# First block of a conditioned residual model: the order of shift, scores and value products on TensorE

## The chip, the cores and the metric

The kernel runs on one core of one Trainium2 chip. The metric is the device time of one execution in microseconds (us). A core has TensorE (PE in the profile, with its weight loads as PEld), VectorE (DVE), ScalarE (ACT), GpSimd (POOL) and SyncE (SP, which here only issues DMAs). Each runs its own list of instructions in order, and they meet through semaphores: an instruction's `then_inc` raises one, a `wait_ge` holds an engine's list until a value is reached.

## The reference

The input x is 16 x 128 x 256. Two layers are added to it in turn.

The first is a masked self-attention in which queries, keys and values are the same projection:

```
x  = x + L0(x, cond)        # 8 heads of 16 channels, T = 256 columns, per batch
  q      = xt @ Wq.T                       # xt: x with its last two axes swapped
  scores = scale * q q^T                   # 256 x 256 per batch and head
  logits = (scores*cmask + (1-cmask)*NEG) * rmask
  ctx    = softmax(logits) q ;  out = ctx @ Wo.T
x  = x + L1(x, cond, ...)   # adaptive layer norm, attention with 16 heads of 128, MLP with gelu
```

The second is a transformer block with modulations computed from cond. It takes most of the time and the change does not touch it.

## The kernel before, in words

`build` runs two parts one after the other: `first_block` (the first layer, and beside it the preparation of the second layer's weights, modulations and first layer norm) and `layers` (the second layer). Each part is written as one list of instructions per engine, and the order in each list is written out by hand.

`first_block` works in 32 units, numbered n = 0 to 31. A unit is two heads (s = 0, 1) of two batches (b = 0, 1). Four units make a group: a group g is the two batches 2g and 2g+1 with all eight heads. The unit's 2 x 2 score tiles live in the four PSUM banks of `ring`: bank 2b + s. So half b of a unit uses banks 2b and 2b+1, and the next unit uses the same banks again.

For half b of unit n:

- `scores(n, b)` (line 446, PE) writes the raw, masked scores of both heads for both key tiles. It waits until the exponentials of unit n-1 have read the same banks (`act_exp`), and at the first unit of a group for the operands QS and KS to be gathered (`l_q`).
- `maxima(n, b)` (line 678, DVE) takes the negated maxima of the two banks, one instruction for each bank.
- `shift(n, b)` (line 458, PE) adds these to the scores in PSUM, by multiplying the maxima with an identity. It waits for `dve_max`, bank by bank.
- `exponentials(n, b)` (line 611, ACT) writes `pt`, one instruction for each bank. `pt` has two buffers, so it waits for the value products of unit n-2 (`pe_pv`).
- `pv(n, kt)` (line 470, PE) is one half (a key tile kt) of the unit's value products: `V` against `pt`, into a 32-row band of the PSUM tile O (`pair`) for each batch and head. It comes a unit late, as `pv(n - 1, ...)` in step n, and needs all four exponentials of its unit (`act_exp` 4n).

The tensor list's step n is: `scores(n, 0)`, `shift(n-1, 1)`, then work that comes once a group, then the first product of unit n-1, `shift(n, 0)`, `scores(n, 1)`, and the second product of unit n-1. The ScalarE list's step n is: `exponentials(n-1, 1)`, copies that come once a group, one cast of 512 columns of the second layer's weights (`w_hi`, line 647, in steps 2 to 25), `exponentials(n, 0)`. In VectorE's list it is `maxima(n, 0)`, group work, `maxima(n, 1)`.

The work once a group, by n mod 4, is this. In steps 0 and 1, ScalarE copies a half of the last group's O (line 619). In steps 1 and 2, PE transposes these (line 514), and VectorE divides by the sums. In step 2, PE projects the queries of the group after next (line 790 with `wq_h`), ScalarE copies them (`qh`, line 594) and VectorE forms their low part (`ql`, line 673). In step 3, PE transposes the contexts (line 521) and projects the next group's values (line 395), which ScalarE copies (line 601). In step 0 PE multiplies with Wo (line 526), and VectorE adds to X (line 772).

The operands of a group go through DRAM. SP stores `qh` and `ql` to `qd` (`gather`, lines 281 and 283), and later, once they have landed, loads them in stacked form into QS and KS (`spread`, line 299). Between these SP loads masks (`mb`, line 272) and weight chunks (`stage`, line 307), the latter when GpSimd is done with the chunk two before.

At steps 28 and 29 ScalarE also computes the row sums and squares of the first layer norm of the second layer (lines 124 and 141), after `exponentials(n, 0)`. After the last unit, PE computes the modulations (line 404), and the last group's contexts are finished.

Of the kernel before, what the change touches and what calls it, by code (L numbers as in the profile page):

```python
# [16 lines left out]
UNITS = B // 2 * 4  # L17
# [26 lines left out]
def wait(eng, sem, value):  # L44

    if not isinstance(value, int) or value > 0:
        eng.wait_ge(sem, value)
# [125 lines left out]
def first_block(nc, sem, sb, x, cond, Wq, Wo, ada_w, ada_b, qkv_w, qkv_b, out_b, ffn_b1, ffn_b2,  # L173
# [10 lines left out]
    with ExitStack() as ctx:  # L184
# [67 lines left out]
        def nth(g):  # L252

            return (g + 1) // 2

        def tail_of(n, lag):

            g, r = divmod(n - lag, 4)
            return g if r == 0 and 0 <= g < NGR else None

        with nc.Block() as block:
# [119 lines left out]
            def _(pe):  # L381
                def project(g):

                    wait(pe, pool_x, g)
                    wait(pe, act_v, g - 1)
                    products(nc, vbank[:, :], lambda k: wq_h[:, :], lambda k: wq_l[:, :], lambda k: xh[:, :],
                             lambda k: xl[:, :], True, True, range(1)).then_inc(pe_q, 1)

                def values(g):

                    taken = min(g + 1, NGR - 1)
                    wait(pe, act_q1, taken)
                    wait(pe, dve_ql, taken)
                    for bk in range(4):
                        last = nc.tensor.matmul(vbank[:, bk * P:(bk + 1) * P],
                                                X[:, 2 * g + bk // 2, bk % 2 * P:(bk % 2 + 1) * P], wT[:, 0, :],
                                                start=True, stop=True)
                    last.then_inc(pe_v, 1)
# [33 lines left out]
                def scores(n, b):  # L432

                    g, j = divmod(n, 4)
                    if g == 0 and b == 0:
                        pe.wait_ge(dve_st, j + 1)
                    elif j == 0 and b == 0:
                        pe.wait_ge(l_q[g % 2], LQ * nth(g))
                    if n == 0 and b == 1:
                        pe.wait_ge(dve_set, 2)  # L440
                    wait(pe, act_exp, 4 * (n - 1) + 2 * b + 2)
                    for kt in range(2):
                        for s in range(2):
                            r = slice(64 * s, 64 * s + ROWS_ONE + 1)
                            k0 = b * 256 + kt * P
                            last = nc.tensor.matmul(ring[:, 2 * b + s, kt * 256:kt * 256 + 256],  # L446
                                                    KS[r, g % 2, j, k0:k0 + P], QS[r, g % 2, j, b * 256:b * 256 + 256],
                                                    start=(kt == 0), stop=True, skip_group_check=True)
                            if kt == 1:
                                last.then_inc(pe_s, 1)  # L450

                def shift(n, b):

                    for s in range(2):
                        wait(pe, dve_max, 4 * n + 2 * b + s + 1)
                        for qt in range(2):
                            out = ring[:, 2 * b + s, :].rearrange("p (k q) -> p k q", k=2)[:, :, qt * P:(qt + 1) * P]
                            last = nc.tensor.matmul(out, mx[:, 2 * b + s, qt:qt + 1].to_broadcast([P, P]),  # L458
                                                    identr[:, None, :].to_broadcast([P, 2, P]),
                                                    start=False, stop=True, skip_group_check=True)  # L460
                        last.then_inc(pe_sh, 1)

                def pv(n, kt):

                    g, j = divmod(n, 4)
                    col = j % 2 * 256
                    for b in range(2):
                        for s in range(2):
                            row = (2 * s + b) * HP
                            last = nc.tensor.matmul(O[row:row + HP, j // 2, col:col + 256],  # L470
                                                    V[:, g % 2, b * 2 + kt, 2 * j + s, :],
                                                    pt[:, n % 2, b, s, kt * 256:kt * 256 + 256],
                                                    start=(kt == 0), stop=(kt == 1))
                    if kt == 1:
                        last.then_inc(pe_pv, 1)
# [16 lines left out]
                for n in range(LAST + 1):  # L492
                    if n < UNITS:
                        scores(n, 0)
                    if 0 <= n - 1 < UNITS:
                        shift(n - 1, 1)
                    if n == 0:
                        pe.wait_ge(act_set, 1)
                        pe.wait_ge(dve_set, 1)
                        project(1)  # L500
                    if n < 3:
                        stack(n + 1)

                    for t in range(2):
                        g = tail_of(n, 5 + t)
                        if g is not None:
                            wait(pe, act_o, 2 * g + t + 1)
                            if t == 0:
                                wait(pe, dve_x, g)
                            else:  # L510
                                wait(pe, dve_ctx, 2 * g + 1)
                            for qt in range(2):
                                for jj in range(2):
                                    last = nc.tensor.transpose(tbank[:, (2 * qt + jj) * P:(2 * qt + jj + 1) * P],
                                                               oT[:, t, (2 * jj + qt) * P:(2 * jj + qt + 1) * P], ident)
                            last.then_inc(pe_oT, 1)
                    g = tail_of(n, 7)
                    if g is not None:
                        wait(pe, dve_ctx, 2 * g + 2)
                        for i in range(4):  # L520
                            last = nc.tensor.transpose(tbank[:, i * P:(i + 1) * P], ctxs[:, i, :], ident)
                        last.then_inc(pe_ctxT, 1)
                    g = tail_of(n, 8)
                    if g is not None:
                        wait(pe, act_ctxT, g + 1)
                        nc.tensor.matmul(tbank[:, :], wT[:, 1, :], ctxT, start=True, stop=True).then_inc(pe_out, 1)
                    if n % 4 == 2 and n // 4 + 2 < NGR:
                        project(n // 4 + 2)
                    if n % 4 == 3 and n // 4 + 1 < NGR:
                        values(n // 4 + 1)  # L530

                    if 0 <= n - 1 < UNITS:
                        if (n - 1) % 4 == 0:
                            wait(pe, act_v, (n - 1) // 4 + 1)
                        if (n - 1) % 2 == 0:
                            wait(pe, act_o, (n - 1) // 2 - 1)
                        wait(pe, act_exp, 4 * n)
                        pv(n - 1, 0)
                    if n < UNITS:
                        shift(n, 0)  # L540
                        scores(n, 1)
                    if n == 0:
                        values(0)
                    if 0 <= n - 1 < UNITS:
                        pv(n - 1, 1)
                    if n == UNITS:
                        pe.wait_ge(act_exp, 4 * UNITS)
                        pe.wait_ge(l_small, 80)
                        nc.tensor.transpose(ring[:, 1, 12 * B:12 * B + BIASES], bias_rows, ident[0:BIASES, 0:BIASES])
                        pe.wait_ge(l_ada, 48)  # L550
                        for part in range(4):
                            modulations(part)
                    if n == UNITS + 1:

                        pe.wait_ge(dve_n1, 1)
                        pe.wait_ge(act_exp, 4 * UNITS)
                        for half in range(2):
                            transposed(nc, ident, normal, half, (vbank, ring[:, 0, :])[half]).then_inc(pe_n1, 1)
# [941 lines left out]
```

## Time and profile before

| | us |
|---|---|
| median of 3 runs | 788.14 |
| lowest, highest | 786.65, 790.93 |
| profiled execution | 792.2 |
| its span in the profile | 790.0 |

The first block takes the span up to about 198 us; the layers take the rest. In the rows below, a line of the timeline merges neighbouring instructions of one kind (x4 is four of them), and gives the start of the first and the time from there to the end of the last. An idle time in brackets stands with what ended it. Lines marked PEld are weight loads. A "..." stands where lines are left out.

### The profile page before, as it was taken

What the parts mean: (1) busy time and instruction counts of PE and PEld (TensorE: products, weight loads), DVE (VectorE), ACT (ScalarE), POOL (GpSimd) and SP (SyncE); (2) the same over time, 40 slices, a digit from 0 to 9 for tenths busy, and PEclk for the clock granted to TensorE, in tenths of its full rate; (3) what the DMA queues carried; (4) which work ended last, traced back from release to release, by engine and by line L of the source; (5) the groups of instructions that cost most, each with busy time, mean ns of one, the idle gap of its engine ahead of it and who ended that gap; (6) DMA issues with size and microseconds to landing.
All of it is one profiled execution on the core that took longest, in us unless ns stands there. A gap on an engine that the chain in (4) does not pass through costs nothing.

```text
span 790.0 us, 12978 instructions
## 1 busy us (share of the span) xinstructions
PE 756.6 (96%) x4763; PEld 621.5 (79%) x4763; DVE 394.5 (50%) x801; ACT 439.5 (56%) x1194; POOL 142.5 (18%) x133
## 2 busy tenths in 40 slices
PE   7799999986999999999999999999999999899997
PEld 4455555555888888888988888988898888778886
DVE  5656666664235534444545443555544435446444
ACT  2557767671465554455655447465454485557653
POOL 4134443100232111111111111111111223200000
PEclk9979999995899999999999999999999999999999
DMA  3989888701332221221212212212222232221001
GB/s 114 180 214 208 214 193 190 143 27 47 126 121 94 68 81 67 68 81 54 80 64 72 80 66 66 71 62 80 81 68 69 69 117 94 67 80 40 30 12 53
DMA packets 67707, 73.30 MB, mean 93 GB/s; under 512 B 3936, under 2 KB 47960, under 8 KB 67656
## 3 DMA queue, kind: packets, MB, share of 16 engines
q1 hardware_dynamic: 67192, 72.40, 32.6%
q8 instruction: 32, 0.52, 0.3%
q10 hardware_dynamic: 464, 0.22, 0.1%
q14 instruction: 19, 0.16, 0.1%
HBM read 46.36 MB, written 26.25 MB: 92 GB/s over the span
## 4 chain that ended last, share of the span: by engine, by line
PE 70%; DVE 3%; ACT 2%; DMA 1%; issue 0%; DVEq 0%; SPq 0%; ACTq 0%
PE bank L790 27%; PE pair L790 14%; PE ring L790 13%; PE ring L1076 7%; PE pair L1062 7%; PE ring L116 1%; DVE x1l L1304 1%; ACT x1h L1164 1%; PE ring L1095 0%; ACT probs L1183 0%; DMA x1f<-in_L_cond_ffn_w_dram 0%; PE ring L1031 0%; DVE ol L1337 0%; DVE pB L1315 0%; DMA turned<-pB 0%
## 5 line engine op out<-in xcount | busy, mean ns | idle before, releaser
L1183 ACT ACTIVATE probs<-pair,nm 128x128 f32<-128x128 f32 x256 | 98.2, 485 | 183.7 <-DVE nm L1326 183.7
L1439 POOL TENSOR_TENSOR probs<-probs,rinv 128x512 f32<-128x512 f32 x64 | 66.6, 1041 | 357.0 <-DVE rinv L1334 357.0
L790 PE MATMUL bank<-x1h,w_hi 128*128 128x512 f32 x256 | 112.1, 438 | 5.6 <-DVE x1l L1304 5.5
L678 DVE TENSOR_REDUCE mx<-ring 128x2 fp32r<-128x512 f32 x128 | 79.8, 683 | 45.1 <-PE ring L446 45.1
L790 PE MATMUL bank<-x1l,w_hi 128*128 128x512 f32 x256 | 101.5, 396 | 0.0
L790 PE MATMUL bank<-x1h,w_lo 128*128 128x512 f32 x256 | 101.3, 396 | 0.0
L611 ACT ACTIVATE pt<-ring 128x512 f32<-128x512 f32 x128 | 70.3, 595 | 45.0 <-PE ring L458 45.0
L1357 DVE COPY Vv<-pair 128x512 f32<-128x512 f32 x64 | 44.2, 691 | 81.0 <-PE pair L790 81.0
L790 PE MATMUL pair<-w_hi,x1l 128*128 128x256 f32 x256 | 72.8, 284 | 0.0
L790 PE MATMUL pair<-w_lo,x1h 128*128 128x256 f32 x256 | 72.6, 283 | 0.0
L790 PE MATMUL pair<-w_hi,x1h 128*128 128x256 f32 x256 | 72.3, 282 | 0.0
L1076 PEld LDWEIGHTS ring<-pT,Vv 128*128 128x128 f32 x512 | 67.7, 193 | 5.2
L1062 PEld LDWEIGHTS pair<-K,Q 128*128 128x128 f32 x512 | 67.0, 191 | 5.3
L1076 PE MATMUL ring<-pT,Vv 128*128 128x128 f32 x512 | 68.2, 276 | 0.0
L1062 PE MATMUL pair<-K,Q 128*128 128x128 f32 x512 | 67.6, 275 | 0.0
L1337 DVE SCALAR_TENSOR_TENSOR ol<-ring,bias,oh 128x512 fp32r<-128x512 f32 x64 | 48.1, 751 | 33.8 <-ACT oh L1192 33.8
L1326 DVE TENSOR_REDUCE nm<-pair 128x4 f32<-128x512 f32 x64 | 43.6, 682 | 40.3 <-PE pair L1062 40.0
L1334 DVE RECIPROCAL rinv<-sums 128x4 f32<-128x4 f32 x64 | 11.4, 178 | 102.0 <-ACT probs L1183 102.0
L790 PEld LDWEIGHTS bank<-x1h,w_hi 128*128 128x128 f32 x256 | 49.1, 192 | 13.6 <-issue 6.6
L790 PEld LDWEIGHTS bank<-x1h,w_lo 128*128 128x128 f32 x256 | 48.6, 190 | 11.0
L1183 ACT ACTIVATION_READ_ACCUMULATOR probs<-pair,nm 128x1 f32 x256 | 56.0, 219 | 0.0
L458 PEld LDWEIGHTS ring<-identr,mx 128*128 128x128 f32 x256 | 37.6, 196 | 22.7 <-issue 13.4
(206 smaller groups left out, 1518.4 us busy)
## 6 DMA issues: line engine op xcount, KB each, us to landing
turned<-pB SPq DMA_DIRECT2D x63, 256.0 KB, 2.0
pT<-turned SPq DMA_DIRECT2D x63, 256.0 KB, 2.7
stage<-in_L_cond_qkv_w_dram SPq DMA_DIRECT2D x12, 512.0 KB, 9.5
QS<-qd SPq DMA_DIRECT2D x14, 384.0 KB
qd<-qh SPq DMA_DIRECT2D x14, 256.0 KB
KS<-qd SPq DMA_DIRECT2D x14, 256.0 KB
mb<-in_cond_dram SPq DMA_DIRECT2D x8, 256.0 KB, 9.6
kept<-X SPq DMA_DIRECT2D x1, 2048.0 KB, 8.0
```

The lines of the kernel that those rows point to most:

```text
L458: last = nc.tensor.matmul(out, mx[:, 2 * b + s, qt:qt + 1].to_broadcast([P, P]), identr[:, None, :].to_broadcast([P, 2, P]), start=False, ...
L611: nc.scalar.activation(pt[:, n % 2, b, s, :], ring[:, 2 * b + s, :], ACT.Exp, scale=DK ** -0.5).then_inc(act_exp, 1)
L678: dve.tensor_reduce(mx[:, 2 * b + s, :], ring[:, 2 * b + s, :].rearrange("p (k q) -> p k q", k=2), AX_X, ALU.max, negate=True).then_inc(dv ...
L790: last = nc.tensor.matmul(bank, w(k), x(k), start=(start and i == 0), stop=(stop and i == len(terms) - 1))
L1062: last = nc.tensor.matmul(Sb[:, t], Q[:, h % 2, t], K[:, h % 2, t], start=True, stop=True)
L1076: last = nc.tensor.matmul(Ob[:, b * T:(b + 1) * T], V[:, ho // 2 % 2, b, h % 2 * DH:(h % 2 + 1) * DH], pT[:, h % 2, :, b, :], start=True, ...
L1183: last = nc.scalar.activation(plain(probs)[:, t] if direct else probs[:, :, b, :].rearrange("p c a -> p a c"), Sb[:, t] if direct else Sb[ ...
L1326: dve.tensor_reduce(nm[:, h % 2, :], Sb[:, :].rearrange("p (b k) -> p b k", b=GB), AX_X, ALU.max, negate=True).then_inc(dve_mx, 1)
L1334: dve.reciprocal(rinv[:, h % 2, :], sums[:, h % 2, :]).then_inc(dve_ri, 1)
L1337: dve.scalar_tensor_tensor(ol[:, :], Ob[:, :], qkvb[:, 2, ho:ho + 1], oh[:, :].bitcast(F32), ALU.add, ALU.subtract).then_inc(dve_ol, 1)
L1357: dve.tensor_copy(V[:, hn // 2 % 2, 2 * (hn % 2):2 * (hn % 2) + 2, :], Vb[:, :].rearrange("p (b d) -> p b d", b=2)).then_inc(dve_v, 1)
L1439: pool.tensor_tensor(w, w, r, ALU.mult).then_inc(pool_p, 1)
```

## The change

In step n of the tensor list, `shift(n, 0)` and `scores(n, 1)` move ahead of the wait for the exponentials of unit n-1 and of the first value product; the second value product, which stood at the end of the step, moves up to stand directly behind the first. No instruction, semaphore or wait is added or taken out, and the other engines' lists are the same. The step is then: `scores(n, 0)`, `shift(n-1, 1)`, work once a group, `shift(n, 0)`, `scores(n, 1)`, both products of unit n-1.

```diff
--- before.py
+++ after.py
@@ -529,6 +529,9 @@
                     if n % 4 == 3 and n // 4 + 1 < NGR:
                         values(n // 4 + 1)
 
+                    if n < UNITS:
+                        shift(n, 0)
+                        scores(n, 1)
                     if 0 <= n - 1 < UNITS:
                         if (n - 1) % 4 == 0:
                             wait(pe, act_v, (n - 1) // 4 + 1)
@@ -536,13 +539,9 @@
                             wait(pe, act_o, (n - 1) // 2 - 1)
                         wait(pe, act_exp, 4 * n)
                         pv(n - 1, 0)
-                    if n < UNITS:
-                        shift(n, 0)
-                        scores(n, 1)
+                        pv(n - 1, 1)
                     if n == 0:
                         values(0)
-                    if 0 <= n - 1 < UNITS:
-                        pv(n - 1, 1)
                     if n == UNITS:
                         pe.wait_ge(act_exp, 4 * UNITS)
                         pe.wait_ge(l_small, 80)
```

## Rows read from the trace of the kernel before

**Rows 1.** The page, busy time, share and instructions of each engine.

```profile
PE 756.6 (96%) x4763; PEld 621.5 (79%) x4763; DVE 394.5 (50%) x801; ACT 439.5 (56%) x1194; POOL 142.5 (18%) x133
```

**Rows 2.** Windows; columns: stretch, length, busy (instructions) per engine, clock, DMA share, GB/s.

```profile
35.00:39.00 4.00, 0.30 (x10) 0.06 (x2) 1.00 (x2) 0.19 (x1) 0.50 (x1) 1.00 1.09 196
...
43.00:47.00 4.00, 4.00 (x24) 2.53 (x23) 2.50 (x4) 2.02 (x4) 3.19 (x4) 0.50 0.60 238
...
70.00:100.00 30.00, 29.15 (x245) 18.36 (x246) 20.13 (x40) 20.86 (x39) 12.01 (x10) 1.00 0.93 205
```

**Rows 3.** Timeline of a group's second unit; start, duration, engine, line, operation, [idle before].

```profile
83.65 2.48 DVE L678 TENSOR_REDUCE mx<-ring 128x2 fp32r<-128x512 f32 x4 [1.06 <-PE ring L446]
...
84.19 0.50 PE L446 MATMUL ring<-QS,KS 49*128 49x256 f32 x4
...
84.62 0.88 PE L458 MATMUL ring<-identr,mx 128*128 128x256 f32 x4
...
85.16 1.08 ACT L611 ACTIVATE pt<-ring 128x512 f32<-128x512 f32 x2 [1.02 <-PE ring L458]
...
85.34 0.60 PE L514 MATMUL bank<-cst,late 128*128 128x128 f32 x4
...
86.39 0.64 PE L470 MATMUL pair<-pt,V 128*32 128x256 f32 x8 [0.45 <-ACT pt L611]
...
86.95 0.73 PE L458 MATMUL ring<-identr,mx 128*128 128x256 f32 x4
...
87.56 1.09 ACT L611 ACTIVATE pt<-ring 128x512 f32<-128x512 f32 x2 [0.32 <-PE ring L458]
...
87.61 0.50 PE L446 MATMUL ring<-QS,KS 49*128 49x256 f32 x4
...
88.69 0.50 PE L446 MATMUL ring<-QS,KS 49*128 49x256 f32 x4
```

**Rows 4.** The same timeline, exponentials of the group's first unit.

```profile
83.05 1.08 ACT L611 ACTIVATE pt<-ring 128x512 f32<-128x512 f32 x2 [0.22 <-PE ring L458]
```

**Rows 5.** The same timeline, cast and exponentials of its third unit.

```profile
91.66 0.62 ACT L647 CAST w_hi<-stage 128x512 fp32r<-128x512 f32 x1
...
92.23 1.08 ACT L611 ACTIVATE pt<-ring 128x512 f32<-128x512 f32 x2
```

**Rows 6.** The same view over units 26 to 31.

```profile
148.41 1.09 ACT L611 ACTIVATE pt<-ring 128x512 f32<-128x512 f32 x2 [1.22 <-PE ring L458]
...
153.28 1.09 ACT L611 ACTIVATE pt<-ring 128x512 f32<-128x512 f32 x2 [0.47 <-PE ring L458]
...
154.51 0.50 PE L446 MATMUL ring<-QS,KS 49*128 49x256 f32 x4
...
157.78 1.09 ACT L611 ACTIVATE pt<-ring 128x512 f32<-128x512 f32 x2 [0.74 <-PE ring L458]
...
162.73 1.09 ACT L611 ACTIVATE pt<-ring 128x512 f32<-128x512 f32 x2 [0.83 <-PE ring L458]
...
168.04 1.08 ACT L611 ACTIVATE pt<-ring 128x512 f32<-128x512 f32 x2 [1.22 <-PE ring L458]
...
172.55 1.08 ACT L611 ACTIVATE pt<-ring 128x512 f32<-128x512 f32 x2 [0.84 <-PE ring L458]
...
174.43 1.19 ACT L611 ACTIVATE pt<-ring 128x512 f32<-128x512 f32 x2 [0.79 <-PE ring L458]
```

**Rows 7.** Timeline: two group heads and the mask load between them.

```profile
98.59 0.51 PE L446 MATMUL ring<-QS,KS 49*128 49x256 f32 x4
...
105.45 0.44 SPq L272 DMA_DIRECT2D mb<-in_cond_dram  x1
...
117.40 0.50 PE L446 MATMUL ring<-QS,KS 49*128 49x256 f32 x4
```

**Rows 8.** DMA issues in 98 to 108; columns: KB each, us from issue to landing.

```profile
mb<-in_cond_dram SPq DMA_DIRECT2D x1, 256.0 KB, 10.4
```

**Rows 9.** Waits of the DMA-issuing queue SP: us in total, times, longest.

```profile
SPq L299 <- DMA qd<-ql: 15.2, 7, 5.8
```

## The prediction

> **What bounds the kernel now.** I read the page first, then the stretches, then the timeline of the first block. On the page TensorE is busy for 96% of the span [rows 1], which seems to leave nothing to reorder. The stretches say the same of the first block (0.97 busy in 70 to 100), and add that the DMA engines are busy for 0.93 of it there [rows 2]. The timeline of one unit says what the busy share hides. I call a unit's blocks S0 and S1 (scores, line 446), T0 and T1 (shifts, 458), P0 and P1 (value products, 470), E0 and E1 (the two pairs of exponentials, 611). The reader is to follow starts, since they show when PE could go on:
>
> S0 84.19, T1 of the unit before 84.62, E1 85.16, four transposes 85.34, then P0 at 86.39 after 0.45 idle for E1, T0 86.95, E0 87.56, S1 87.61, and the next S0 at 88.69 [rows 3]. The next S0 starts 0.04 after E0 ends (87.56 + 1.09 = 88.65). So ScalarE's E0 ends the unit, and ScalarE itself stood idle 0.32 before E0, for T0. T0 had its maxima long before: those of S0 are the last two of the four reductions that start at 83.65; at 2.48 / 4 = 0.62 apart, the third, T0's first, is done near 85.6. T0 stood only behind P0, and P0 behind E1. The loop is E1, P0, T0, E0, S0, T1, E1, through two engines that wait for each other. PE is not the bound; its order is.
>
> **The change, part by part.**
>
> *No instruction is added or removed, and no wait.* All semaphore counts stay. S1's own wait for E1 (act_exp 4n) was satisfied by P0's before; now S1 is the one that waits, and P0 and P1 find it done. No DMA is moved; SP and POOL see only earlier counts.
>
> *T0 ahead of P0.* T0 can start once the transposes and its maxima are done, near 85.8 in the unit of rows 3, instead of 86.95. E0 can then follow the weight cast directly: the idle 0.32 goes. It is the same in the first unit of a group, where ACT idles 0.22 before E0 [rows 4]. In the third unit E0's row has no idle time at all [rows 5], nor has the fourth's: there, as the code's order has it, ScalarE is held by the query copy and the value copy, which wait for projections that stay where they are. These two units gain nothing. So a group gains 0.22 + 0.32 = 0.54 (the bounds: 0, if T0 is held by something else, and 0.45 more in the second unit, P0's own wait).
>
> *S1 ahead of P0 and P1.* S1 waits for E1 (ends 86.24), then P0 and P1 follow. P0 takes 0.57 (86.39 to 86.95), S 0.43 (84.19 to 84.62), T 0.66 (86.95 to 87.61). PE's own path through a unit is 2 x 0.43 + 2 x 0.66 + 2 x 0.57 = 3.3, with the transposes (0.4 to 0.6) 3.8. That is the price: both products now stand between S1 and the next S0. In the second unit of a group ScalarE needs 88.69 - 84.19 - 0.32 = 4.2, so 0.4 is spare. Where ScalarE has no cast or copy to do, the 3.8 becomes the bound and eats part of what the wait gave.
>
> *The two products together.* They no longer switch between kinds of matmul in between. No row of before shows an uninterrupted pair; the nearest, P0's 0.57 to the next block, bounds a pair at 1.14, and 0.43 (an S block's) would make it 1.00. From -0.14 to 0 a unit, and only where PE is the bound; I take 0.
>
> *Where it adds up.* Counted by unit (0 to 31):
> - Units 0 to 3 wait for the operand stacks on VectorE and then for the gathers; nothing. Units 4 to 7 run partly at half clock [rows 2], where PE's own path is the longer one: between 0 and 0.54, I take 0.2.
> - Units 8 to 23, four groups of 0.54: 2.2. Units 24 and 25: 0.5.
> - Units 26 and 27 have no cast; ACT idles 1.22 and 0.47 before E0 [rows 6]. PE's path caps this: the sum is 1.7 at most, 0 at least; unit 26 keeps some 0.7 and unit 27, which has the value projection on PE, some 0.2. I take 0.9.
> - Units 28 to 31, where the layer norm's sums and squares run on ScalarE between the exponentials: idle 0.74, 0.83, 1.22 and 0.84 before E0 [rows 6], 3.6 together. Every one of these waits is for T0 behind P0 behind E1. The last unit's products come after E1 as before, so what PE's path takes here falls mostly in the shade of the squares. I take 3.3; the ends are 2.3 (0.3 a unit to PE's path) and 3.6.
>
> Sum without transfers: 0.2 + 2.2 + 0.5 + 0.9 + 3.3 = 7.1.
>
> *What the faster loop runs into.* Each group's first S0 waits for gathers through DRAM. For the head at 117.40 the mask load, issued behind the gathers at 105.45, landed 10.4 later, at 115.85 [rows 7, 8]. The gathers should have landed by then, so 1.5 was left; the sum has taken 0.2 + 3 x 0.54 = 1.8 by that head and 3.8 by the head of unit 28. SP waited for the operands' stores to land in all 7 gathers, 15.2 in total [rows 9], so this chain of transfers is little helped by earlier compute, at 0.93 busy engines [rows 2]. If it moves not at all, 2.3 of the 3.8 is lost; if it moves along, 0. I take 1.0, nearer to moving, since the weight loads that share the engines are issued earlier as well. Sum: **6.1**.
>
> The Trainium skill ("DMA: Bandwidth & Descriptors", Queues, rings and completion order) says that each DMA engine takes descriptors in ring order but that completion isn't first in, first out per issuing engine. By it the bound of 115.85 is a likely one and no certain one; by the rows alone the 1.5 stays as it is.
>
> After unit 31 (modulations, transposes, the start of the layers) the chain moves as a whole; PE's clock there may change level a little earlier or later in it, 0.5 either way. The layers are untouched.
>
> The profiled execution took 792.2 (span 790.0 and 2.2 around it), 4.1 above the median of 788.14. 792.2 - 6.1 = 786.1 for it, and 782.0 for the median.
>
> **The rivals.**
>
> *A: the transfers take it all (chance 0.16).* The gathers hold every head, so units 4 to 27 end where they did, and only the tail's 3.3 is left: 784.8. For it: 0.93 busy DMA engines, SP's waits. Against: 1.5 was left at the head I could date, and no full-speed head shows a measured wait.
>
> *B: slower (0.07).* PE, done sooner, waits at the heads long enough to lose its clock. That has happened once: in 35 to 39 PE was busy for 0.30 of 4 us (the wait for the first gathers), and in 43 to 47 the clock was 0.50, the level of 1.2 GHz [rows 2]. At that level the path of 3.8 doubles to near 7.6 against units of 4.5, so one such head costs about 3 a unit and 6 in two units. That wait was 3.7, and I take the rival to decide from a wait of that order; the sum above has heads wait under 1.5. With two such heads and the tail's gain: 788.1 - 3.3 + 12 = 796.8; one, with the rest of A, makes 790.8, and I write 791 for the rival.
> The Trainium skill ("TensorE: Matmul & The Clock Gate", HAM oscillation) describes just this: a wait for transfers in each round throttles the array again every round. Here the trace agrees at the one long wait; by the rule this rival would strike wherever a wait is as long as that one.
>
> *C: the wait only moves (0.07).* S1 waits for E1 as P0 did, and P0 and P1 between S1 and S0 cost what T0 gained: 788. Against it: in the unit of rows 3, T0 at 85.8 puts S1 at 86.5 and the pair from 86.9 to 88.0, before E0 ends (88.65 - 0.32 = 88.3).
>
> *D: more than forecast (0.10).* Transfers move along, and units 26 and 27 give their whole 1.7 because the pair of products is cheap: 7.1 + 0.8 = 7.9; and where E0 follows a cast with no idle it starts 0.05 before the cast ends (92.23 against 91.66 + 0.62 [rows 5]), in ten units 0.5 more: 8.4, so 779.7.
>
> **How the numbers follow.** The forecast (gain 4.5 to 8, 0.60): 782.0. A median of this kernel can tell about 0.5%, 3.9, from no change. Faster by more: forecast and D, 0.70. Within: A and C, 0.23. Slower: B, 0.07. The range is from 778.5 (D, with a microsecond of spread) to 786.5 (A, with half a microsecond of clock and one of spread), and leaves C, B and the far side of D outside.
>
> **What would show it.** Right: ACT's idle time for line 458 falls in first and second units; PE waits for E1 at S1, none at P0; the distance of group heads (98.59 to 117.40, 18.81 [rows 7]) falls toward 18.3; E1 of the last unit starts some 6 earlier than 174.43 [rows 6]. In the third and fourth unit of a group nothing changes. Wrong: group heads that stay at 18.8 with PE waiting for DMA (A); a clock of 0.50 after a head (B); E0 as late as before although T0 is early (C). The tail's share can be read apart: from the S0 at 154.51 to E1 at 174.43 it is 19.92 now [rows 6], and should be near 16.6.

## The result, and the profile after

Nine runs of each kernel: 784.72 us after against 788.73 before, ratio 0.9924 with a 95% interval of 0.990 to 0.9948; that is 6.0 faster, between 4.1 and 7.9. The gains in this text come from these ratios; differences of the medians can be smaller, and here the two medians are only 4.0 apart. The forecast was a gain of 6.1 and a median of 782.0; the measured median is 2.7 above that, inside the stated range (778.5 to 786.5). One of the twelve executions of the kernel called "end alone" below took 1830.47, in a slow state, and is not in its ratio. The profiled execution took 785.6, with a span of 783.4, against 792.2 and 790.0.

The page of the kernel after, busy time of each engine. It looks like [rows 1]: PE's (TensorE's) busy share went from 96% to 95% while the kernel gained 6. The Trainium skill ("Perfetto Trace Analysis", Identifying the Most-Contended Engine) warns that matmul busy time is a poor measure of how close TensorE is to its limit; here the rows agree.

```profile
PE 745.7 (95%) x4763; PEld 623.4 (80%) x4763; DVE 396.4 (51%) x801; ACT 437.2 (56%) x1194; POOL 142.4 (18%) x133
```

The timeline after, a group's second unit. It answers to [rows 3]; columns as there.

```profile
64.35 0.50 PE L446 MATMUL ring<-QS,KS 49*128 49x256 f32 x4 [0.16 <-ACT pt L610]
...
64.79 0.74 PE L458 MATMUL ring<-identr,mx 128*128 128x256 f32 x4
...
65.32 1.09 ACT L610 ACTIVATE pt<-ring 128x512 f32<-128x512 f32 x2 [1.02 <-PE ring L458]
65.36 0.60 PE L514 MATMUL bank<-cst,late 128*128 128x128 f32 x4
...
65.72 1.02 PE L458 MATMUL ring<-identr,mx 128*128 128x256 f32 x4
...
66.66 0.50 PE L446 MATMUL ring<-QS,KS 49*128 49x256 f32 x4
66.76 0.64 ACT L646 CAST w_hi<-stage 128x512 fp32r<-128x512 f32 x1
67.10 1.07 PE L470 MATMUL pair<-pt,V 128*32 128x256 f32 x16
67.28 1.11 ACT L610 ACTIVATE pt<-ring 128x512 f32<-128x512 f32 x2
68.44 0.50 PE L446 MATMUL ring<-QS,KS 49*128 49x256 f32 x4 [0.28 <-ACT pt L610]
```

T0 starts at 65.72, right behind the transposes. E0 at 67.28 has no idle time before it; it starts 0.12 before the cast ends (66.76 + 0.64). The products are one block at 67.10 and lie beside E0. The unit is 4.09 long (64.35 to 68.44), where it was 4.50. E0's end still sets the next S0, and PE now has 0.28 idle there.

The first unit of the next group shows the other side. I call the first S0 of a group its head. Timeline after, then windows (columns as in [rows 2]):

```profile
76.68 1.07 PE L470 MATMUL pair<-pt,V 128*32 128x256 f32 x16
...
79.37 0.50 PE L446 MATMUL ring<-QS,KS 49*128 49x256 f32 x4 [1.62 <-DMA QS<-qd]
```

```profile
78.00:79.00 1.00, 0.00 (x0) 0.00 (x0) 0.07 (x1) 0.00 (x0) 0.34 (x1) 1.00 0.99 154
...
81.00:82.00 1.00, 1.00 (x3) 0.49 (x3) 0.35 (x2) 1.00 (x3) 0.91 (x2) 0.50 0.90 344
82.00:83.00 1.00, 1.00 (x8) 0.78 (x6) 0.54 (x1) 1.00 (x3) 0.95 (x1) 0.50 0.59 223
...
85.00:86.00 1.00, 1.00 (x11) 0.87 (x10) 0.70 (x2) 0.27 (x1) 0.00 (x0) 1.00 0.46 133
```

PE had nothing to do from 77.75 to 79.37; the gathers had not landed. Then its clock was at 0.50 (1.2 GHz) in 81 to 83 and at 1.00 again in 85 to 86, and the unit took 5.39 in place of 4.09. Before, no head but the first gathered one (38.95) waited for a transfer.

SP's wait for the stores to land is longer than in [rows 9]; waits of SP after:

```profile
SPq L299 <- DMA qd<-ql: 23.5, 7, 6.8
```

The issues themselves show what became of the earlier compute. First stores of a group's queries and the gathers that wait for them, timeline before, then after:

```profile
73.02 1.27 SPq L281 DMA_DIRECT2D qd<-qh  x2
...
84.00 0.81 SPq L299 DMA_DIRECT2D KS<-qd  x2
```

```profile
71.43 1.27 SPq L281 DMA_DIRECT2D qd<-qh  x2
...
84.85 0.81 SPq L299 DMA_DIRECT2D KS<-qd  x2
```

The stores were issued 1.6 earlier and the gathers 0.85 later. Over the five groups issued from 53 to 130, the time from the first store to the first gather was 10.0 to 11.8 before and 11.7 to 13.4 after.

The end of the block, timeline after (answers to [rows 6]):

```profile
153.07 0.50 PE L446 MATMUL ring<-QS,KS 49*128 49x256 f32 x4 [1.34 <-DMA QS<-qd]
...
162.70 2.03 ACT L610 ACTIVATE pt<-ring 128x512 f32<-128x512 f32 x4
...
169.53 1.08 ACT L610 ACTIVATE pt<-ring 128x512 f32<-128x512 f32 x2 [0.76 <-PE ring L458]
```

Unit 28's head gained 1.44 (154.51 to 153.07). From there to the last E1 it took 16.46, where it was 19.92, so 3.46 more. At 162.70 four exponentials stand in one row without idle time, E1 of unit 29 and E0 of unit 30: the squares of the layer norm hold ScalarE, and when they end both are ready.

Then the stretch from the modulations to the layers, which gives the last 1.5 of the 6.6 between the two spans. Windows of the kernel before and of the one after:

```profile
176.80:197.80 21.00, 14.47 (x75) 12.09 (x71) 9.15 (x34) 3.72 (x7) 0.00 (x0) 0.57 0.15 49
```

```profile
171.70:191.30 19.60, 13.03 (x76) 10.66 (x72) 9.22 (x34) 3.72 (x7) 0.00 (x0) 0.62 0.16 54
```

The same work with a mean clock of 0.62 against 0.57. By their starts (first modulation to first product of the layers) it was 176.89 to 197.84, and is 171.85 to 191.28: 1.5 shorter. PE's clock fell to 0.50 about 3 after the first modulation before, and about 4.5 after it here.

### The profile page after: what moved, and what is told of

The parts are those of the page before. It is cut to its first block, busy times and chain, and to the rows that moved or that the text cites. A ratio compares the mean times of both kernels' runs of the same rounds, so it can differ in the third digit from the quotient of the medians.

```text
span 783.4 us, 12978 instructions
## 1 busy us (share of the span) xinstructions
PE 745.7 (95%) x4763; PEld 623.4 (80%) x4763; DVE 396.4 (51%) x801; ACT 437.2 (56%) x1194; POOL 142.4 (18%) x133
## 4 chain that ended last, share of the span: by engine, by line
PE 70%; DVE 3%; ACT 2%; DMA 1%; issue 0%; DVEq 0%; SPq 0%; ACTq 0%
PE bank L789 28%; PE pair L789 14%; PE ring L789 13%; PE ring L1075 7%; PE pair L1061 7%; PE ring L116 1%; DVE x1l L1303 1%; ACT x1h L1163 1%; PE ring L1094 0%; ACT probs L1182 0%; DMA x1f<-in_L_cond_ffn_w_dram 0%; PE ring L1030 0%; DVE ol L1336 0%; DVE pB L1314 0%; DMA turned<-pB 0%
## 5 line engine op out<-in xcount | busy, mean ns | idle before, releaser
L677 DVE TENSOR_REDUCE mx<-ring 128x2 fp32r<-128x512 f32 x128 | 81.7, 685 | 37.4 <-PE ring L446 37.0
L458 PE MATMUL ring<-identr,mx 128*128 128x256 f32 x256 | 55.3, 329 | 1.8 <-DVE mx L677 0.5
```

The costliest lines, as they stand in the source:

```text
L677: dve.tensor_reduce(mx[:, 2 * b + s, :], ring[:, 2 * b + s, :].rearrange("p (k q) -> p k q", k=2), AX_X, ALU.max, negate=True).then_inc(dv ...
```

## The experiments

Each time is a median beside that of the kernel before on the same chip; the gain is the ratio's, and the medians themselves differ by up to 1.2 less. For the traces I give the heads of groups 2 to 7 (first S0 of units 8, 12, ..., 28) and the start of the last unit's S1. Before they are 60.96, 79.78, 98.59, 117.40, 136.21, 154.51 and 172.61; after 60.26, 79.37, 98.54, 116.39, 135.41, 153.07 and 167.56.

**Only T0 moved.**

```diff
+                    if n < UNITS:
+                        shift(n, 0)
                     if 0 <= n - 1 < UNITS:
...
                         pv(n - 1, 0)
                     if n < UNITS:
-                        shift(n, 0)
                         scores(n, 1)
```

> Only the first shift T0 stands ahead of the first value product; the second scores S1 stay between the two products. Theory 1 (the gain is E0 of the unit starting without waiting for P0 and E1): nearly all of the change's gain of 6.0 (0.76% of 788.7) is here, 4.5 to 6, since E0 needs T0 alone; in the trace ACT's idle time before E0 is gone in first and second units and a group's second unit is near 4.1 long. Theory 2 (S1 ahead and the closed pair of products carry a good part, because PE's own path and the maxima of S1 bound the units): 3 or less.

785.46 against 789.56, ratio 0.9939 (0.9915 to 0.9962): 4.8 faster. Timeline of its first and second unit behind a head:

```profile
83.97 1.00 PE L458 MATMUL ring<-identr,mx 128*128 128x256 f32 x4
...
84.90 0.64 PE L470 MATMUL pair<-pt,V 128*32 128x256 f32 x8
84.90 0.64 ACT L648 CAST w_hi<-stage 128x512 fp32r<-128x512 f32 x1
85.42 1.11 ACT L612 ACTIVATE pt<-ring 128x512 f32<-128x512 f32 x2
85.47 0.50 PE L446 MATMUL ring<-QS,KS 49*128 49x256 f32 x4
85.90 0.64 PE L470 MATMUL pair<-pt,V 128*32 128x256 f32 x8
86.58 0.50 PE L446 MATMUL ring<-QS,KS 49*128 49x256 f32 x4
```

E0 follows the cast as it does after, and the unit is 4.08 long: T0 ahead is the whole of it here. S1 and the closed pair are worth 0.1 in the third unit (4.57 against 4.48) and 0.16 to 0.3 in units without a cast (unit 26: 3.96 against 3.75; unit 28: 4.00 against 3.84; unit 30: 4.07 against 3.77). From unit 28's head to the last S1 this kernel took 15.72, the old order 18.10 and the change 14.49: of the tail's 3.6, T0 gives 2.4, and S1 with the pair 1.2. No run tells S1 from the pair. Theory 1 for the body, and for two thirds of the tail.

**Only the pair closed**, ahead of T0.

```diff
                         pv(n - 1, 0)
+                        pv(n - 1, 1)
                     if n < UNITS:
                         shift(n, 0)
                         scores(n, 1)
...
-                    if 0 <= n - 1 < UNITS:
-                        pv(n - 1, 1)
```

> The two products stand together, but ahead of T0 and S1, as the first did before. Theory 1: the pair (1.0 instead of 0.57) now lies between E1 and E0, 0.43 more in each ACT-bound unit, 28 units: 8 to 12 slower than before, 797 to 801. Theory 2 (the pair itself is worth something): within 3 of before.

799.99 against 789.56, ratio 1.0138 (1.0095 to 1.0182): 10.9 slower. Timeline, a group's first unit:

```profile
83.68 1.07 PE L470 MATMUL pair<-pt,V 128*32 128x256 f32 x16
...
84.68 0.73 PE L458 MATMUL ring<-identr,mx 128*128 128x256 f32 x4
85.27 1.08 ACT L610 ACTIVATE pt<-ring 128x512 f32<-128x512 f32 x2 [0.65 <-PE ring L458]
```

A pair takes 1.00 to the next block, 0.43 more than one product, and all of that is added to ScalarE's idle time: 0.22 [rows 4] became 0.65. So what PE does between E1 and E0 is on the path at full price.

**The end alone, and the rest alone.**

```diff
+                    early = n >= 28      # the other kernel: n < 28
+                    if early and n < UNITS:
+                        shift(n, 0)
+                        scores(n, 1)
...
                         pv(n - 1, 0)
-                    if n < UNITS:
+                    if not early and n < UNITS:
                         shift(n, 0)
                         scores(n, 1)
```

> The new order in steps 28 to 32 only, the old one before. Theory 1 (the tail of the block, where the layer norm's sums stand on ScalarE and no gathers are due, gives 3.6 as the two traces show): 3 to 4.5 faster than before, and the time from the head of unit 28 to the last exponentials as short as after. Theory 2 (the gain comes evenly from all units, 4 of 32): under 1.5.

> The new order in steps 0 to 27 only, the old one from 28. Theory 1 (the gathers hold the heads of the groups): 1 to 2 faster than before, head of unit 28 near 153, from there as before. Theory 2 (body and tail share the gain by the number of their units): 4 to 5 faster.

Theory 1 held for the end, and for the rest in its size but not in the head it named (near 153). End alone: 786.19 against 789.56, ratio 0.9949 (0.9926 to 0.9972), 4.0 faster. From unit 28's head to the last S1 it took 14.49, as after, where it was 18.10: 3.6 gained.

Rest alone: 788.20, ratio 0.9982 (0.9961 to 1.0003), 1.4 faster at best estimate and not told from nothing. Its heads: 59.92, 77.80, 95.67, then 114.81, 135.25, 154.27. After two groups of 17.9 it was 2.9 ahead of before, and the next three gave all but 0.2 back: two heads waited 1.65 and 2.55 for gathers, and behind the second wait PE ran at half clock. Timeline at that head, and the windows behind the two waits:

```profile
135.25 0.80 PE L446 MATMUL ring<-QS,KS 49*128 49x256 f32 x4 [2.55 <-DMA QS<-qd]
```

```profile
115.00:119.00 4.00, 3.74 (x34) 2.20 (x32) 3.21 (x5) 2.92 (x6) 2.21 (x3) 1.00 0.79 305
...
135.25:141.25 6.00, 6.00 (x26) 3.85 (x30) 2.71 (x5) 3.16 (x6) 1.28 (x1) 0.50 0.46 152
```

Unit 24, behind 135.25, took 6.84 in place of 4.09.

**Less transferred beside the gathers.** The two kernels leave out 7/8 of the qkv weights from the third chunk on, so the products of the layers use stale weights.

```diff
+                    w = CHUNK if c < 2 else 128
-                    sp.dma_start(stage[:, c % 2, :], qkv_v[:, k, n * CHUNK:(n + 1) * CHUNK])...
+                    sp.dma_start(stage[:, c % 2, 0:w], qkv_v[:, k, n * CHUNK:n * CHUNK + w])...
```

> Old order; from the third chunk on, the transfers of the qkv weights bring only 128 of 1024 columns (the rest of the product weights is left stale), so ten transfers of 512 KB shrink to 64 KB. If the old order is bound by the loop of engines and not by transfers at the heads of groups 3 to 7: the same distances of heads (18.8), total within 2 of before except for what the first gathers, which wait for transfers, give (0 to 2).

> New order with the same lightened weight transfers. Theory 1 (transfers hold the heads in the new order): PE's waits for gathers at the heads go, heads at 17.9 to 18.3 apart, and the gain over the light kernel in the old order is 7 to 8.5 instead of 6. Theory 2 (the gathers' own chain, not the weights beside it, or something else sets the heads): same distances as after, gain over the light old order near 6.

Old order: ratio 1.0003 (0.9974 to 1.0032), heads 18.8 apart as before. New order: 0.9854 (0.9803 to 0.9904), 11.5 faster; heads at 60.03, 79.20, 97.07, 114.94, 132.81, 149.07, with three distances of 17.87. Only the head at 60.03 waited for a gather (1.59), and its unit took 5.39. The gain over the light old order is 11.8 by these ratios, more than the 7 to 8.5 expected; why it is more stays open. The transfers held the new order and not the old one.

**One store less.** The high part of the queries goes to DRAM once, and both stacks are loaded from it: 256 KB less written a group, and two loads more to issue.

```diff
-    LQ, LG = 10 * 16, 3 * 16
+    LQ, LG = 12 * 16, 2 * 16
...
-                    for c in (0, 2):
-                        sp.dma_start(q[:, c], qh[:, :].bitcast(F32)).then_inc(l_qd[g % 2], 16)
+                    sp.dma_start(q[:, 1], qh[:, :].bitcast(F32)).then_inc(l_qd[g % 2], 16)
...
-                    sp.dma_start(q[:, 1], ql[:, :].bitcast(F32)).then_inc(l_qd[g % 2], 16)
+                    sp.dma_start(q[:, 0], ql[:, :].bitcast(F32)).then_inc(l_qd[g % 2], 16)
...
-                        for dst, r, c, n in ((KS, 0, 1, 2), (KS, 2, 0, 1), (QS, 0, 0, 3)):
+                        for dst, r, c, n in ((KS, 0, 0, 2), (KS, 2, 1, 1), (QS, 0, 1, 1), (QS, 1, 0, 2)):
-        qd = nc.dram_tensor("qd", (2, NH, 3, DK, 512), F32).ap()
+        qd = nc.dram_tensor("qd", (2, NH, 2, DK, 512), F32).ap()
```

> Old order; the high part of the queries is stored to DRAM once and not twice, and both stacks are loaded from the one copy (256 KB less written a group, two more small-row loads to issue). If the old order is bound by the loop: full-speed heads as before, 18.8 apart; the one long wait for the first gathers at 35 to 39 gets shorter, so 0 to 4 faster than before, more if the clock no longer falls there.

> New order with the single store. Theory 1: the stores and gathers form a chain of their own of some 18 to 19 a group, and 256 KB less makes it shorter: PE's waits at the heads fall to near 0, 7 to 10 faster than before. Theory 2 (bytes stored are no part of what holds the heads): as after, 6 faster.

Old order: 788.24 against 790.38, ratio 0.9964 (0.9938 to 0.9991), 2.8 faster; its heads are 18.8 apart, and what it gained up to the head of unit 28 (1.7) came with the first gathers, whose head fell from 38.95 to 36.73.

New order: **775.78 against 790.38, ratio 0.980 (0.9759 to 0.9842), 15.8 faster than before**, and the best version here. Two of its heads in the timeline:

```profile
94.27 0.50 PE L445 MATMUL ring<-QS,KS 49*128 49x256 f32 x4 [0.38 <-ACT pt L609]
...
112.14 0.50 PE L445 MATMUL ring<-QS,KS 49*128 49x256 f32 x4 [0.38 <-ACT pt L609]
```

They are 17.87 apart and wait for ScalarE, not for a transfer. SP now waits for the stores twice, for 5.6 together, where after it was seven times, for 23.5. All heads: 58.53, 76.40, 94.27, 112.14, 129.99, 146.25. Its span, 774.1, is 15.9 below before: 8.3 up to unit 28, 3.6 in the tail, and 3.7 in the stretch of the modulations, which is the part that varies. The expectation said 7 to 10, which was too low. The two changes bring more together than the sum of each alone (6.0 and 2.8): the new order makes the transfers the bound, and the single store moves that bound away.

**One store more.**

```diff
-                    for c in (0, 2):
+                    for c in (0, 2, 3):
```

(with `qd` one slot larger and LG = 4 * 16)

> Old order with one more store of the queries' high part, into a slot that nothing reads (256 KB more written a group). If the chain of stores and gathers had 1 to 2 to spare a group in the old order, as its one dated head says, the longer chain now holds the heads: distances above 18.8, PE waits for gathers, 2 to 8 slower than before. If transfers had ample room: heads 18.8 apart, within 2 of before.

> New order with the same extra store. Theory 1 (in both orders the chain of transfers then sets the heads): the distances equal those of the old order with the extra store, near 20, and only the tail's 3.6 stands between the two, so the change's gain shrinks from 6 to 3 to 4.5. Theory 2 (heads set by the engines' loop in the new order too): gain stays near 6 or more.

Old order: ratio 1.0058 (1.003 to 1.0086), 4.6 slower; heads 80.80, 99.75, 119.82, 139.87, 158.50, two of them 20.1 apart. New order: 0.9996 (0.9973 to 1.002), so the change's gain is 4.9 there by the two ratios and 3.8 by the medians; heads 81.41, 99.28, 119.32, 138.87, 158.06. At unit 28 the two orders stand 0.44 apart (158.50 and 158.06). So both orders are held to nearly the same heads, as theory 1 has it. The last S1 is 2.84 apart (176.62 and 173.78), with 2.4 of it from the tail and not the 3.6 expected: unit 28 of the new order ran at half clock behind its wait (5.40 long). Theory 1 named a gain of 3 to 4.5 and theory 2 one near 6; 4.9 lies between, and it is the heads that decide. SP's waits for the stores add up to 31.3 and 34.0 in these two.

**The kernel after once more.**

> The changed kernel once more, for a second profile. If the 1.5 that its first profile shows between the modulations and the layers is the clock's luck: that stretch is anywhere in 17.2 to 21.3, as in the kernels run so far, while unit lengths without waits for gathers are the same to 0.05 (4.09, 4.09, 4.48, 5.21 in a group) and head distances vary.

One run, 782.76, span 780.6. Units without a wait: 4.09, 4.08, 4.48 and 5.21, as in the first profile. Heads: 59.34, 78.31, 96.19, 116.41, 135.62, 152.59. Another head now had the long wait:

```profile
116.41 0.52 PE L446 MATMUL ring<-QS,KS 49*128 49x256 f32 x4 [2.72 <-DMA QS<-qd]
...
116.86 1.22 PE L458 MATMUL ring<-identr,mx 128*128 128x256 f32 x4
```

```profile
118.00:120.00 2.00, 2.00 (x5) 0.97 (x4) 0.42 (x2) 1.77 (x4) 1.85 (x3) 0.50 0.55 215
```

From the first modulation to the layers it took 18.9. The thirteen profiles have 17.2 to 21.3 there (21.0 before, 19.4 after, 17.2 with a store less in the old order, 17.3 in the new), and either order has both short and long ones.

## Why the prediction was right

**The loop was the bound, and T0 ahead of P0 opened it**: shown by T0 alone (0.9939), and from the other side by the pair alone (1.0138). That part of the prediction is right in its mechanism. That its sum came near the measured 6.0 is in part luck: what the order can give in units 8 to 27 was 2.2 too small and what the transfers take 4.1 too small, units 0 to 7 and the tail gave 0.8 more, and so 5.0 came out in place of 6.1.

**The terms.** The kernel with one store less shows what the order gives when no transfer holds it. Against [rows 3] and [rows 6]:

| term | predicted | shown without transfers | of it realised after |
|---|---|---|---|
| full group, units 8 to 23, each | 0.54 | 0.94 (18.81 to 17.87) | |
| units 24 and 25 | 0.5 | 0.7 | |
| units 26 and 27 | 0.9 | 1.3 (4.42 to 3.75, 4.96 to 4.33) | |
| units 8 to 27 together | 3.6 | 5.8 | |
| the same, less transfers | 2.6 | | 0.7 |
| units 0 to 7 | 0.2 | | 0.7 |
| units 28 to 31 | 3.3 | 3.6 | 3.6 |

Two sizes were off, in opposite directions. *T0 ahead of P0* was too small: I took the idle times of [rows 3, 4], 0.32 and 0.22. The units gained 0.41 and 0.32, because E0 overlaps the end of the cast by 0.1 once it doesn't wait; rival D had half of that. And "these two units gain nothing" failed for the third, which gained 0.20 (4.68 to 4.48). In it T1 no longer waits for its second maximum, because S1 of the unit before is earlier: the part of S1 that I had not counted. T1 stands ahead of the query projection in PE's list, and ScalarE's query copy waits for that. Timeline before, then after; the copy starts 2.48 after its unit's S0 (88.69), then 2.33 (68.44):

```profile
89.13 0.87 PE L458 MATMUL ring<-identr,mx 128*128 128x256 f32 x4
...
91.17 0.58 ACT L594 CAST qh<-bank 128x512 fp32r<-128x512 f32 x1 [0.42 <-PE bank L790]
```

```profile
68.88 0.73 PE L458 MATMUL ring<-identr,mx 128*128 128x256 f32 x4
...
70.77 0.59 ACT L593 CAST qh<-bank 128x512 fp32r<-128x512 f32 x1 [0.27 <-PE bank L789]
```

With T0 alone the third unit is 4.57, so about half of the 0.20 is T0's.

*What the faster loop runs into* was too small as well, and by more: from the head of unit 8 to that of unit 28 the kernel took 93.55 before and 92.81 after, 0.7 of the 5.8 that the order can give. The gathers took 5.1 of it, 1.3 of that through the half clock behind one wait, where I had predicted 1.0. The step that failed is "nearer to moving, since the weight loads that share the engines are issued earlier as well". The chain of stores and gathers did not move along: the stores were issued up to 1.6 earlier, and the gathers behind them at nearly the old times (84.85 against 84.00, 103.56 against 102.70, 122.88 against 122.22). The heads stayed near 19 apart, and with 256 KB more they were 20 apart. The forecast that the distance of 18.81 falls toward 18.3 held for one of four groups (19.1, 19.2, 17.9, 19.0), and the last E1 started 4.9 earlier, not 6.

The 1.5 that I took as left to the transfers came from the one head that I had dated. The same reading at the head of 79.78 gives less; timeline and issues before:

```profile
68.72 0.44 SPq L272 DMA_DIRECT2D mb<-in_cond_dram  x1
```

```profile
mb<-in_cond_dram SPq DMA_DIRECT2D x1, 256.0 KB, 10.2
```

The mask behind those gathers landed at 78.96, 0.8 ahead of the head, and the one behind the gathers of 60.96 (issued at 51.55, 9.4 later) at the head itself.

Rival A was nearly the truth for the body (rest alone: 1.4 at best). Its "only the tail's 3.3 is left" is close to what the kernel with the end alone measured, 4.0. The profiled execution gained 6.6 because the tail gave 3.6, the heads 1.4 and the stretch of the modulations another 1.5, which varies from run to run; the first two are the change's, 5.0 together, inside the measured 4.1 to 7.9 and 1.1 below the forecast.

**Rival B** was priced too high and its threshold set too far. "I take the rival to decide from a wait of that order", 3.7, failed: matmuls idle for 1.62 at 79.37 and for 2.72 at 116.41 (second profile) were followed by half clock. But it lasted 3 to 4 us there and cost 1.3 each time (5.39 and 5.44 in place of 4.09), not 6. Before, behind the wait of 3.7, it had lasted 10:

```profile
40.00:50.00 10.00, 9.17 (x52) 5.26 (x50) 4.10 (x9) 5.51 (x11) 5.66 (x5) 0.50 0.74 260
```

The dearest case of a gathered head behind unit 8 is that of rest alone: 7 us at half clock, 2.75 lost (6.84 in place of 4.09). It made the gain smaller and did not turn it. The Trainium skill ("TensorE: Matmul & The Clock Gate", HAM oscillation) says that a wait for transfers in each round throttles the array each time; after, matmuls idled for a gather at five heads (38.99, 60.26, 79.37, 135.41, 153.07), and two of them, 38.99 and 79.37, were followed by half clock, so here it was some rounds and not every one.

**Rival C** fell: P0 and P1 lie beside E0. The pair costs 1.00 to the next block where two single ones cost 1.14, the end of the range that I had not taken. **Rival D** had the right sign for the body (the cast's overlap, more in units 26 and 27), and what it assumed of the transfers was wrong.

What stays open is why the heads are 17.9 apart in one group and 20 in the next in the same kernel. With less weight traffic, and with one store less, the later heads stood 17.87 apart, so the stores and what shares the DMA engines with them are shown to matter; how they delay one another is not shown. Whether the stretch of the modulations is shorter for a reason in the new order is not shown either: thirteen profiles don't point that way.

## What to carry to other kernels

An engine that is busy for 96% can still be one whose order, and not its work, is the bound: follow the starts around one turn of the loop, find the instruction whose inputs were ready long before, and look at what stands ahead of it in its queue. When a loop gets faster, date the transfers that feed it, in every turn and not in one: if they have less to spare than the gain adds up to, the gain goes there, and the cheapest next step is on their side. Here one store less was worth 2.8 with the old order and some 10 behind the new one (15.8 less 6.0).

## What the runs showed of the hardware

Matmuls idle for 1.57 (one store more, new order, at 158.06), 1.59 (light new order, at 60.03), 1.62 (after), 2.04 and 3.40 (one store more, new order, at 138.87 and 61.03), 2.55 (rest alone) and 2.72 (second profile of after) were followed by a clock of 0.50, at the latest 1.6 us after they went on. Idle times of 1.22 at 135.41 and 1.34 at 153.07 (after) were not, but neither were 1.65 at 114.81 (rest alone) and 2.54 at 119.32 (one store more, new order). So the length of the wait alone does not tell. The window behind that last one:

```profile
119.30:123.30 4.00, 3.92 (x34) 2.38 (x34) 3.01 (x5) 3.01 (x6) 2.71 (x3) 1.00 0.80 315
```

The half clock lasted 3 to 4 us in five of these seven, and near 7 us behind the 2.55 and the 3.40. One product block takes 0.57 to the next block of another kind, two in a row 1.00.
